# Layer norms of six batch fronts moved from VectorE to ScalarE in a two-layer recurrent and mixture-of-experts kernel

## What is computed

```python
def _layernorm(x, axis=-1, eps=1e-05):
    m = jnp.mean(x, axis=axis, keepdims=True)
    v = jnp.var(x, axis=axis, keepdims=True)
    return (x - m) / jnp.sqrt(v + eps)
...
    x = L0_attn_x
    xn = _layernorm(x, axis=-1)
    s = _L0_attn_ref(xn, ...)          # selective scan, 16 states, 256 channels
    g = _silu(_L0_ffn_ref(xn, ...))    # 8 experts, top 2, and a shared one
    x = x + s * g
    xn = _layernorm(x, axis=-1)
    s = _L1_attn_ref(xn, ...)          # products of queries and combiners
    g = _silu(_L1_ffn_ref(xn, ...))    # 8 experts, top 2, and a shared one
    x = x + s * g
```

## Time and profile before

| what | value |
| --- | --- |
| median of 3 runs | 1181.41 us (1178.0 to 1184.15) |
| the profiled execution | 1182.9 us, span 1181.1 us, mean granted clock 0.87 |
| VectorE (DVE) | 960.9 us busy |
| TensorE (PE) | 916.1 us busy |
| ScalarE (ACT) | 608.5 us busy |
| GpSimd (POOL) | 592.5 us busy |

### The profile page before, as it was taken

How to read it: one execution, slowest core, us unless ns; L and a number is a source line. 1 busy time by engine, 2 the same in 40 slices (tenths; PEclk the granted TensorE clock), 3 DMA queues, 4 the chain that set the end, 5 groups by cost and what they waited for, 6 DMA issues and landing times.

```text
span 1181.1 us, 16955 instructions
## 1 busy us (share of the span) xinstructions
PE 916.1 (78%) x4540; PEld 650.3 (55%) x4540; DVE 960.9 (81%) x1811; ACT 608.5 (52%) x1593; POOL 592.5 (50%) x415
## 2 busy tenths in 40 slices
PE   3475687967767778868888888888768888898588
PEld 1343475645645655656656565656546565566455
DVE  3797889899889897987999978998479877876463
ACT  2444545654545555545575556654455455555133
POOL 1348226657427544781358543765848365226300
PEclk9576889988888998998999899998887889889677
DMA  9944335456344534563536534566454464445000
GB/s 280 294 119 127 87 89 123 118 126 186 86 100 120 125 90 114 150 183 91 114 99 151 132 93 117 133 189 147 114 124 93 103 169 114 104 91 146 21 24 13
DMA packets 168650, 144.71 MB, mean 123 GB/s; under 512 B 15680, under 2 KB 135536, under 8 KB 168560
## 3 DMA queue, kind: packets, MB, share of 16 engines
q10 hardware_dynamic: 39776, 67.47, 26.1%
q1 hardware_dynamic: 121104, 60.43, 18.0%
q0 software_dynamic: 7680, 15.74, 4.2%
HBM read 106.88 MB, written 36.70 MB: 122 GB/s over the span
## 4 chain that ended last, share of the span: by engine, by line
PE 35%; DVE 33%; issue 14%; ACT 9%; POOL 6%; DMA 1%; ACTq 1%; another core or an unknown queue 1%; DVEq 0%; SPq 0%; POOLq 0%
DVE pA L1352 11%; PE pM L935 6%; PE pH L845 4%; PE pM L925 4%; DVE hj L1388 4%; POOL dBx L748 3%; PE pG L897 3%; PE p L900 3%; PE pU L898 3%; DVE hj L1400 2%; ACT pA L955 2%; DVE hc L1360 2%; PE pG L900 2%; PE pH L913 2%; POOL rows_in L706 1%
## 5 line engine op out<-in xcount | busy, mean ns | idle before, releaser
L748 POOL TENSOR_TENSOR dBx<-dtx,bcb 128x1024 f32<-128x1024 f32 (+1 forms) x144 | 304.6, 2115 | 403.6 <-DVE pA L1352 387.0
L845 PE MATMUL pH<-const,hc 128*128 128x128 f32 x1024 | 160.9, 304 | 43.4 <-DVE hc L1360 38.9
L1352 DVE TENSOR_TENSOR_SCAN pA<-pA,carry,dBx 128x512 f32<-128x512 f32 (+1 forms) x160 | 162.9, 1063 | 30.9 <-ACT pA L955 24.9
L955 ACT ACTIVATE pA<-dt,am 128x512 f32<-128x512 f32 (+1 forms) x288 | 173.9, 639 | 17.6 <-DVE hc L1360 9.4
L1352 DVE TENSOR_TENSOR_SCAN pA<-pA,dBx 128x512 f32<-128x512 f32 x128 | 149.8, 1216 | 27.9 <-ACT pA L955 11.7
L925 PE MATMUL pM<-const,hj 128*128 128x128 f32 (+3 forms) x636 | 131.9, 305 | 44.3 <-ACT hT L1138 10.7
L845 PEld LDWEIGHTS pH<-const,hc 128*128 128x128 f32 x1024 | 128.1, 156 | 64.3 <-DVE hc L1360 46.1
L1360 DVE TENSOR_TENSOR hc<-pA,bcb 128x1024 f32<-128x1024 f32 (+1 forms) x144 | 159.3, 1106 | 5.0
L706 POOL DMA_INDIRECT rows_in<-xn,slots x120 | 127.8, 1065 | 30.1 <-issue 27.0
L925 PEld LDWEIGHTS pM<-const,hj 128*128 128x128 f32 (+3 forms) x636 | 74.0, 141 | 118.9 <-issue 88.7
L1135 ACT ACTIVATE yj<-pM 128x128 f32<-128x128 f32 x236 | 65.4, 277 | 140.1 <-PE pM L935 125.0
(11 more groups left out here) (201 smaller groups left out, 1533.5 us busy)
## 6 DMA issues: line engine op xcount, KB each, us to landing
bcb<-bc_rows ACTq DMA_DIRECT2D x112, 512.0 KB
rows_out<-yj SPq DMA_DIRECT2D x236, 64.0 KB
xg<-rows_in SPq DMA_DIRECT2D x176, 64.0 KB
bcb<-bc_rows ACTq DMA_DIRECT2D x32, 256.0 KB
rows_in<-gy SPq DMA_DIRECT2D x8, 512.0 KB, 8.9
mixed<-s_st SPq DMA_DIRECT2D x12, 256.0 KB
so<-rows_out SPq DMA_DIRECT2D x6, 512.0 KB
sr<-mixed SPq DMA_DIRECT2D x6, 512.0 KB
```

Source lines behind the costliest of these rows:

```text
L748: pool.tensor_tensor(dBx[:, N % 2, :, 0:t1 - t0], dtx[q % 2][:, :, t0:t1], row, ALU.mult).then_inc(dBx_ready, 1)
L845: last = mm(pH[:, half, c * DI + k * P:c * DI + (k + 1) * P], hc[:, N % 2, k, t * P:(t + 1) * P], ident, is_transpose=True, start=(n == 0 ...
L955: A(pA[:, k, 0:t1 - t0], dt[q % 2][:, k, t0:t1], ACT.Exp, scale=am[:, k, n:n + 1]).then_inc(decay_ready, 1)
L1352: dve.tensor_tensor_scan(pA[:, k, 0:w], pA[:, k, 0:w], dBx[:, N % 2, k, 0:w], carry[:, k, N % NS:N % NS + 1] if N in carry_after else 0.0, ...
```

## The change

In the six full-width fronts other than (0,0) the two statistics instructions per tile are replaced. VectorE reduces the source to a sum per token in one TENSOR_REDUCE and scales it to a negative mean. ScalarE squares (x - mean) tile by tile, with the accumulator output giving the sum of squares of a token; each square waits for the one before, as all write the same scratch tile. Four squares stand in step s ("sq" 0) and four in step s + 1 ("sq" 1). VectorE's "var" in step s + 1 waits for all eight and makes variance + eps; GpSimd's root stands at "var" now. "shift" (s + 2) multiplies the negative mean by rstd. ScalarE then writes xn = x * rstd + shift, four tiles in step s + 2 and four in s + 3, and the wait for the previous scatters goes with them. All that follows in the front is one step later, and the due steps with it. TensorE's first transposes wait for the first four tiles.

```diff
--- before.py
+++ after.py
@@ -74,6 +74,11 @@
     return (l, b) in ((0, 0), (0, 1), (0, 2), (1, 0))
 
 
+def norm_on_act(l, b):
+
+    return (l, b) != (0, 0) and cols(l, b) == (0, CT)
+
+
 def make_plan():
 
 
@@ -89,7 +94,16 @@
     def front(l, b, s, per_step):
 
         at(s, "norm", l, b)
-        at(s + 1, "xn", l, b)
+        if norm_on_act(l, b):
+            at(s, "sq", l, b, 0)
+            at(s + 1, "sq", l, b, 1)
+            at(s + 1, "var", l, b)
+            at(s + 2, "shift", l, b)
+            at(s + 2, "xn", l, b, 0)
+            at(s + 3, "xn", l, b, 1)
+            s += 1
+        else:
+            at(s + 1, "xn", l, b)
         at(s + 2, "xT", l, b, 0)
         if cols(l, b) == (0, CT):
             at(s + 3, "xT", l, b, 1)
@@ -309,6 +323,7 @@
         if it[0] == "combine" and it[3] == 0:
             combos.append(it[1:3])
     front_no = {f: n + 1 for n, f in enumerate(fronts)}
+    act_front_no = {f: n for n, f in enumerate(f for f in fronts if norm_on_act(*f))}
     combo_no = {f: n for n, f in enumerate(combos)}
     pool_combo_no = {f: n for n, f in enumerate(f for f in combos if on_pool(*f))}
     sg_no = {f[1]: n + 1 for n, f in enumerate(f for f in fronts if f[0] == 1)}
@@ -382,6 +397,10 @@
         xnT = {(0, b): x0T[b % 2] for b in range(NB)}
         x1T = sb("x1T", [P, L])
         xnT.update({(1, b): x1T if b < LAST else x0T[0] for b in range(NB + 2)})
+        xsum = sb("xsum", [P, CT])
+        negmean = sb("negmean", [P, CT])
+        ssq = sb("ssq", [P, CT])
+        squares = sb("squares", [P, P])
         stats = sb("stats", [P, CT, 6])
         mv = sb("mv", [P, CT, 2])
         vpe = sb("vpe", [P, CT])
@@ -510,6 +529,7 @@
         xn_first, decay_negated = sem("xn_first"), sem("decay_negated")
         bank_full, bank_read = sem("bank_full"), sem("bank_read")
         gate_full = sem("gate_full")
+        mean_ready, ssq_ready, shift_ready, xn_half = sem("mean_ready"), sem("ssq_ready"), sem("shift_ready"), sem("xn_half")
         x_in, stats_ready, rstd_ready, xn_ready = sem("x_in"), sem("stats_ready"), sem("rstd_ready"), sem("xn_ready")
         zl_ready, el_ready, picked_ready, slots_ready, sg_ready = (
             sem("zl_ready"), sem("el_ready"), sem("picked_ready"), sem("slots_ready"), sem("sg_ready"))
@@ -679,7 +699,7 @@
                     pool.memset(gy[:, 0], 0.0).then_inc(zero_tile, 1)
                     pool.memset(bd[:], 0.0)
                     pool.memset(bdw[:], 0.0).then_inc(zero_tile, 1)
-                elif kind == "norm" or (kind, *a) == ("xn", 0, 0):
+                elif kind == "var" or kind == "norm" and not norm_on_act(*a) or (kind, *a) == ("xn", 0, 0):
                     F = front_no[tuple(a)]
                     c0, c1 = cols(*a)
                     if F == 1:
@@ -771,6 +791,8 @@
                     l, b, m = a
                     if (l, b, m) == (0, 0, 0):
                         pe.wait_ge(xn_first, 1)
+                    elif norm_on_act(l, b) and m == 0:
+                        pe.wait_ge(xn_half, act_front_no[l, b] + 1)
                     else:
                         pe.wait_ge(xn_ready, front_no[l, b])
                     take(*("xT", *a))
@@ -968,6 +990,26 @@
                     act.dma_start(const[:], T["const"]).then_inc(const_loaded, 16)
                     act.dma_start(cw[:], T["L0_attn_conv_w"].rearrange("(k p) j -> p k j", p=P)).then_inc(conv_loaded, 16)
                     act.dma_start(cb[:], T["conv_b"]).then_inc(conv_loaded, 16)
+                elif kind == "sq":
+                    l, b, m = a
+                    src = x if l == 0 else xr
+                    act.wait_ge(mean_ready, act_front_no[l, b] + 1)
+                    done = CT * act_front_no[l, b]
+                    for c in range(HT * m, HT * (m + 1)):
+                        if done + c:
+                            act.wait_ge(ssq_ready, done + c)
+                        A(squares[:], src[:, c, :], ACT.Square, bias=negmean[:, c:c + 1], accum_out=ssq[:, c:c + 1]
+                          ).then_inc(ssq_ready, 1)
+                elif kind == "xn" and norm_on_act(*a[:2]):
+                    l, b, m = a
+                    src = x if l == 0 else xr
+                    act.wait_ge(shift_ready, act_front_no[l, b] + 1)
+                    if m == 0:
+                        pl, pb = fronts[front_no[l, b] - 2]
+                        act.wait_ge(scattered[pl][pb % 2], 16 * TOPK * CT * (pb // 2 + 1))
+                    for c in range(HT * m, HT * (m + 1)):
+                        last = A(xn[:, c, :], src[:, c, :], ACT.Identity, scale=rstd[:, c:c + 1], bias=negmean[:, c:c + 1])
+                    last.then_inc(xn_ready if m else xn_half, 1)
                 elif kind == "xT":
                     l, b, m = a
                     act.wait_ge(bank_full, use["xT", l, b, m])
@@ -1190,7 +1232,10 @@
                     src = x if l == 0 or b >= LAST else xr
                     if l == 0:
                         dve.wait_ge(x_in, 16 * (b + 1))
-                    if (l, b) == (0, 0):
+                    if norm_on_act(l, b):
+                        link(dve.tensor_reduce(xsum[:], src[:], op=ALU.add, axis=AX))
+                        dve.tensor_scalar(negmean[:], xsum[:], -1.0 / P, None, ALU.mult).then_inc(mean_ready, 1)
+                    elif (l, b) == (0, 0):
                         moments(src, 0, HT)
                         dve.wait_ge(stats_ready, 1)
                         dve.wait_ge(rstd_ready, 1)
@@ -1201,7 +1246,15 @@
                         dve.wait_ge(conv_scaled, 1)
                     else:
                         moments(src, *cols(l, b))
-                elif kind == "xn":
+                elif kind == "var":
+                    l, b = a
+                    dve.wait_ge(ssq_ready, CT * (act_front_no[l, b] + 1))
+                    dve.tensor_scalar(vpe[:], ssq[:], 1.0 / P, EPS, ALU.mult, ALU.add).then_inc(stats_ready, 1)
+                elif kind == "shift":
+                    l, b = a
+                    dve.wait_ge(rstd_ready, front_no[l, b] + 1)
+                    dve.tensor_tensor(negmean[:], negmean[:], rstd[:], ALU.mult).then_inc(shift_ready, 1)
+                elif kind == "xn" and not norm_on_act(*a[:2]):
                     l, b = a
                     F = front_no[l, b]
                     src = x if l == 0 or b >= LAST else xr
```

## The result

The changed kernel takes 1205.6 us (median of 4 runs, 1197.8 to 1214.9), the kernel before 1181.8 us; the ratio is 1.0243, with a 95% interval of 1.0191 to 1.0296. So it costs 24 us. The forecast was 1189 and a range up to 1199: the direction was right, the size a third of what came, and the time lies outside the range.

What follows compares the result with a forecast made beforehand. No engine is full; VectorE (81%) and TensorE (78%) are near it, in a ring of waits with ScalarE. Terms summed to 10.4 us, a quarter off gave +8 on the 1181.4 median: 1189 us, range 1170 to 1199.

Steps and rivals of the forecast that it cites:

- The deciding term: In step s+1 VectorE's var waits for all eight squares, going on 5.5 us after hc instead of 2.1 us.
- The shift of the scan two steps on: Per front, how much later the scan of state s+2 starts: from +0.4 us at (0,2) to +3.0 at (0,1).
- Rival B: TensorE sets the pace at the fronts, so var's wait is mostly covered: -10 us, 1171; chance 0.25.
- small operations with an idle time ahead: Sign: VectorE's small operation after the squares idles 3 to 5 us, released by ScalarE, in at least five fronts.
- the tile's wait of under 3 us: Sign: TensorE's wait for the first routed tile of (1,0) shrinks from 8.0 us to under 3.
- The stall at step 65: Routed tiles of (1,0) start at 67, not 65: stall goes, -5.3 us, 1.5 come back, net -4.
- The later step as a whole: Planner's fronts one step longer: -4 us from the stall at step 65, +2 from a job done at the end.
- The slack that I counted for five fronts: Jobs of five fronts are used later than due; only routed tiles of (1,0), due and started at 65, have none.
- The tail's +2: The job lost at step 65 is done in the last step, 1.6 us at the high clock, twice at the low; +2.
- Tiles on ScalarE: Steps s+2 and s+3: 1.6 us each delay tanh or flip copies; ScalarE's waits for TensorE cover it, else 19 us.
- Small operations at 0.18 us: Three new small VectorE operations a front, priced as the variance's; with the reduction 10.8 us added, some 21 us net relief.
- The discount of a quarter: A quarter off the 10.4 us sum, as not all of a VectorE stall lasts; leaves +8 us.

Runs made afterwards that it cites:

- e1_shift: Kernel before, norms and tiles still on VectorE, but transposes, routing, scatters and due steps of the six fronts one step later; ratio 1.0069.
- e5_due: Kernel before with no stage moved, only the due steps of the six fronts' expert jobs one later; ratio 1.0059.
- e12_pin: Changed kernel with both transposes in s+3 and all behind them where it stood before the change; ratio 1.0268.
- e13: Kernel before with the change in fronts (1,1) and (1,2) alone; ratio 1.0169.
- e14: Kernel before with the change in fronts (0,1), (0,2) and (0,3) alone; ratio 1.0149.
- e6: Kernel before with the stages behind the tiles one step later in front (1,2) alone; ratio 1.0009.
- e4: Kernel before with only the normalised tiles moved to ScalarE, four in step s+1 and four in s+2, nothing later; ratio 1.0018.
- e10: Kernel before with the six fronts normalising only one of their eight tiles, the other seven left out; ratio 0.9921.
- e3: Changed kernel with squares on ScalarE but the eight normalised tiles on VectorE in step s+2; ratio 1.0317.
- e2: Changed kernel with all eight squares in step s; ratio 1.0052.
- e9: Changed kernel with each square of the second four done twice; ratio 1.0305.
- e16_change: The changed kernel itself measured once more; ratio 1.0294.

## Why the prediction failed, step by step

**What held.** The deciding term was the wait. The squares were estimated at 0.50 us from a copy, a pointer operand and an unknown read-out; they stand 0.53 apart, 0.40 for the square and 0.19 for a read-out instruction, overlapping by a little. The shift of the scan two steps on was forecast +2.8, +2.7, +1.5, +0.4 for (1,0), (1,1), (1,2), (0,2) and came to +3.0, +2.9, +0.7, +0.1. Rival B, with the wait covered, had demanded squares done within 3.2 us of hc; the shortest wait that VectorE had was 3.70 us. For (0,1) I had +3.9 and a later 0.9 back: it was +5.0, since VectorE was free at 120.7 and the variance could start only at 129.38, an idle time of 8.68 us. In the steps up to 50 this is made good, which I had not forecast; the lag there is below nothing. It isn't the wait that is worked off: e1_shift, which has no such wait, gains 7.7 us in the same steps, e5_due, with due steps alone, gains nothing there, and e12_pin, with the wait and without the later step, loses 2.4 from step 13 to 50. So the gain comes from the later stages. Of the signs named, small operations with an idle time ahead in all six fronts came true (8.7, 3.9, 6.0, 5.0, 8.1 and 3.7 us), and the tile's wait of under 3 us didn't.

**The stall at step 65 (term of -4 us).** Wrong in sign; this is the step of the prediction that failed worst. I took the first routed tile to be fetched quietly once its job started at 67, with 1.5 us to come back of the 5.3 saved. The first half was nearly right: the lag falls by 3.5 us at step 67, and by 6.1 in e5_due, which has no squares. What comes back is 7.4 us by step 69 (8.4 in e5_due) in place of 1.5. Of the two 512 KB transfers that had gone out just ahead of the loads, SyncE's fetch is gone at the new place, but the load of bcb is there, and TensorE waits 7.41 us in place of 7.96. Net +3.8 where -4 stood: 8 us of the miss. That the load of bcb is what holds up the tile was not tried.

**The later step as a whole (-4 + 2 us).** e5_due makes it +7, e1_shift +8. The slack that I counted for five fronts was right: in e13 and e14 every job stands in its old step. The sixth front pays, by the stall and by a lane that runs a job behind. That isn't all of it, as the traces of e1 and e6 show: the stages themselves gain 7.7 us up to step 50 and lose 6 to 7 between steps 104 and 114, and I had both at nothing. The tail's +2 can't be seen in the profile of the change, whose tail was 93.7 us against 97.8: it had the higher clock, 0.85 against 0.76. At nearly the same clock e5's tail (0.82), with the job moved, is 94.9 us and e4's (0.83), without, 92.2, so +2 was about right.

**Tiles on ScalarE (2 us).** Taken at a tenth of 19 us, as ScalarE is 52% busy and often waits for TensorE. e4 against e10 makes it 11.4 us, so in e4 the cover that I named is for the most part not there. In the changed kernel the price was not measured by itself; e3 shows only that the tiles on VectorE would cost 8 to 10 us more. I take the reason to be that ScalarE's idle time lies ahead of copies that TensorE releases late, and that 1.6 us put in front of them moves the copies and TensorE's next product. That is argued; the sums of waits of e4 and e10 don't tell them apart there.

**Small operations at 0.18 us.** The held tiles went and small operations are held in their place:

```profile
L1350 DVE COPY xs<-xs 128x6 f32<-128x6 f32 x4 | 5.0, 1250 | 0.0
L1237 DVE TENSOR_SCALAR negmean<-xsum 128x8 f32<-128x8 f32 x6 | 3.8, 625 | 0.2
L1256 DVE TENSOR_TENSOR negmean<-negmean,rstd 128x8 f32<-128x8 f32 x6 | 3.7, 620 | 0.0
L1236 DVE TENSOR_REDUCE xsum<-x 128x8 f32<-128x1024 f32 x3 | 3.6, 1209 | 0.0
L1252 DVE TENSOR_SCALAR vpe<-ssq 128x8 f32<-128x8 f32 x6 | 1.0, 171 | 35.3 <-ACT squares L1001 35.3
```

These are lines of VectorE's operations by shape in the changed kernel. The copy of six elements took 164 ns before; now four take 5.0 us, three of them 1.5 to 1.7 us each. With the two other small ones that is 9.6 us held, where the tiles had been held 4.8 us. That is most of the difference between the 21 us that VectorE was to shed and the 9.9 it did. The reduction was 1.21 us, as estimated (1.22).

**The discount of a quarter.** I took it off the shifts left over at the fronts, as if the lag would shrink again. It grew: the shifts two steps on add up to 11.7 us, with the 3.8 at the moved stall to 15.5, and the lag ends at 24.0. The experiments don't bear the discount out as a rule either. A piece of wait passes on at 0.7 of its length between e2 and the change and at 0.9 to 1.0 in the scan of e9, and e10 gives 0.7 of VectorE's work with an interval from a third to all. With 0.7 for everything the measured pieces come near the result: 35.3 us of wait x 0.73 = 26, 11 for the tiles and 7 for the later step, less what VectorE's 32 us of shed statistics and tiles give (some 23 at 0.7), is 21 us. That sum is put together after the fact and isn't a test.

**Unsettled.** VectorE's wait for dBx rose from 11.6 to 17.6 us. The trace shows what the longest stands behind. SyncE's three fetches of 512 KB for batch 0 of layer 1 wait for xn of (1,2) and go out at 844.19, before at 814.46, so 30 us later where the lag is 22. Then a store of yj lands late, and GpSimd waits for it with the gathers that stand in its queue ahead of dBx:

```profile
852.34 0.98 POOL L742 DMA_INDIRECT w13a<-rows_out,slots  x1 [6.61 <-DMA rows_out<-yj]
...
860.81 2.35 POOL L768 TENSOR_TENSOR dBx<-dtx,bcb 128x1024 f32<-128x1024 f32 x1
863.20 2.35 DVE L1405 TENSOR_TENSOR_SCAN pA<-pA,dBx 128x512 f32<-128x512 f32 x2 [4.91 <-POOL dBx L768]
```

That the fetches delay the store was not tried. Nor is it a loss that can be seen: the lag is 21.5 us at step 104 and 19.7 at step 107, behind this wait. Which stages make the lag grow behind (1,1) is open, as is the value of the move with no wait at all. Fewer squares at a time, or squares ahead of the xs copies, were not tried either.

## What to carry to other kernels

A moved operation costs what the receiver's queue looks like at that place, and its share of busy time doesn't tell: ask what stands ahead of it in that queue and what stands behind the wait in the giver's. If the giver must wait for the answer, leave it a full step of other work in between; here one word (the second squares a step earlier) was worth 22 us of 24, and what is left of the move gains nothing. And a transfer that a schedule change seems to avoid has to be looked for at its new place: a load issued just before its use stays one. A stage that is moved by one step can gain in one part of a run and lose in another; the lag by step shows both, where the total shows their balance.

## What the runs showed of the hardware

- A square with accumulator output is two instructions in the trace, ACTIVATE 0.40 us and ACTIVATION_READ_ACCUMULATOR 0.19 us, for a 128x128 tile; with a wait for the one before they follow each other every 0.53 us. No table load was added for the squares: there are 17 in either kernel.
- Small VectorE operations can be held as long as large ones: a COPY of 6 elements 1.60 us at 286.15 and a TENSOR_TENSOR of 8 elements 2.85 us at 296.25, both while GpSimd was multiplying. The copy ends at 287.75 and GpSimd's product of dBx at 287.72; the other ends at 299.10 and GpSimd's product of gy at 299.07. The Trainium skill (SBUF — State Buffer, Who interferes with whom) names copy and tensor_scalar, and two-input operations, as those that share a port pair with GpSimd; these rows agree, and show that the price doesn't shrink with the operation.
- The same program's tail took 93.7 us in one execution and 99.6 in another, with the clock that TensorE was granted in it at 0.85 and 0.76 (the changed kernel and e16_change), a spread as large as most effects sought here.
